# One order of the token stage for another, and one product moved from VectorE to GpSimd, in an audio tower kernel

## The reference

```python
ww = u + kt; q = maximum(pp, ww)
e1 = exp(pp - q); e2 = exp(ww - q)
y = (e1 * a + e2 * vt) / (e1 * b + e2)
ww2 = pp + w; q2 = maximum(ww2, kt)
e1b = exp(ww2 - q2); e2b = exp(kt - q2)
a, b, pp = e1b * a + e2b * vt, e1b * b + e2b, q2
```

## Time and profile before

| | us |
|---|---|
| median of 3 runs | 1123.95 (1120.25 to 1124.64) |
| the profiled execution | 1119.51 |
| its span, first to last instruction | 1117.4 |
| busy over the span: TensorE, VectorE, ScalarE, GpSimd | 947.9, 819.9, 618.0, 516.2 |
| mean granted clock of TensorE | 0.913 |

### The profile page before, as it was taken

One profiled execution on the slowest core, in us unless ns is written; L12 is line 12 of the kernel. 1 busy time (PEld: TensorE's weight loads), 2 busy tenths in 40 slices (PEclk: granted clock), 3 DMA queues, 4 the chain that ended last, 5 costly groups with the idle time before them and its releaser, 6 DMA issues. The chain is left out here.

```text
span 1117.4 us, 19101 instructions
## 1 busy us (share of the span) xinstructions
PE 947.9 (85%) x5742; PEld 791.6 (71%) x5742; DVE 819.9 (73%) x2076; ACT 618.0 (55%) x1150; POOL 516.2 (46%) x462
## 2 busy tenths in 40 slices
PE   6787788778885531999999999999999999999994
PEld 4454555445553421899899899899899899899894
DVE  2678887888877862778778778778778778778762
ACT  2766777667766512456456456456456456456441
POOL 1003443224422354257557557557557557547524
PEclk9888879887987655999999999999999999999997
DMA  9223443334211144356456456456456456456413
GB/s 295 68 85 93 126 109 97 87 100 135 89 43 29 43 43 175 118 154 168 134 147 176 132 147 173 132 146 174 132 146 174 132 148 172 134 153 168 133 25 38
DMA packets 72695, 138.98 MB, mean 124 GB/s; under 512 B 11949, under 2 KB 63790, under 8 KB 68682
## 3 DMA queue, kind: packets, MB, share of 16 engines
q0 software_dynamic: 31136, 98.34, 33.3%
q1 hardware_dynamic: 41514, 40.08, 12.8%
HBM read 110.52 MB, written 27.86 MB: 124 GB/s over the span
## 5 line engine op out<-in xcount | busy, mean ns | idle before, releaser
L1092 ACT ACTIVATE hid<-hp,b 128x512 f32<-128x512 f32 (+1 forms) x248 | 158.5, 639 | 302.8 <-PE hp L1127 295.0
L1139 PE MATMUL acc<-whi,hhi 128*128 128x256 f32 x880 | 245.9, 279 | 0.0
L1139 PE MATMUL acc<-whi,hlo 128*128 128x256 f32 x880 | 245.9, 279 | 0.0
L1139 PE MATMUL acc<-wlo,hhi 128*128 128x256 f32 x880 | 245.3, 279 | 0.0
L1223 DVE CAST hhi<-hid 128x512 fp32r<-128x512 f32 (+1 forms) x248 | 106.9, 431 | 148.4 <-ACT hid L1092 147.7
L1054 POOL DMA_INDIRECT out_rows<-yout,dest x110 | 180.0, 1636 | 63.7 <-issue 52.0
L1127 PE MATMUL hp<-xhi,whi 128*128 128x512 f32 (+1 forms) x496 | 187.8, 379 | 10.0 <-DVE xlo L1170 7.6
L1127 PE MATMUL hp<-xlo,whi 128*128 128x512 f32 (+1 forms) x496 | 184.0, 371 | 0.0
L1127 PE MATMUL hp<-xhi,wlo 128*128 128x512 f32 (+1 forms) x496 | 183.8, 371 | 0.0
L1139 PEld LDWEIGHTS acc<-wlo,hhi 128*128 128x128 f32 x880 | 165.3, 188 | 9.0
L1068 ACT ACTIVATE whi<-raw 128x512 fp32r<-128x512 f32 x248 | 154.3, 624 | 31.5 <-DMA raw<-in_ew,idx 31.5
(11 more groups left out here) (187 smaller groups left out, 1463.4 us busy)
## 6 DMA issues: line engine op xcount, KB each, us to landing
xin<-in_x SPq DMA_DIRECT2D x32, 512.0 KB
xin<-in_x SPq DMA_DIRECT2D x32, 256.0 KB
token_rows<-xs SPq DMA_DIRECT2D x16, 259.0 KB, 2.6
out_rows<-h SPq DMA_DIRECT2D x16, 256.0 KB, 2.5
token_rows<-xs SPq DMA_DIRECT2D x32, 64.8 KB, 2.4
out_rows<-h SPq DMA_DIRECT2D x32, 64.0 KB, 2.1
xg<-token_rows,tid POOLq DMA_INDIRECT x110, 2.9
out_rows<-yout,dest POOLq DMA_INDIRECT x110, 4.0
```

Source lines behind the costliest of these rows:

```text
L1092: act.activation(hid[:, c % 2, 0:j.r * P], hp[c % 2][:, 0:j.r * P], ACT.Relu, bias=b1[:, j.s, c:c + 1]).then_inc(hid_done, 1)
L1139: last = pe.matmul(acc_of(j, r), h_[:, c % 4, r * P:(r + 1) * P], w_[:, j.s, at:at + C], start=c == 0 and n == 0 and r % 2 == 0, stop=c == ...
```

## The change

- GpSimd gets the product e2sv = es[:, 1] * v, ahead of the seeds of the round and so behind the six list writes of the round before. It counts on a semaphore of its own, `product`, for which VectorE's sa scan waits. VectorE's L654 goes, and N_STATE becomes 6.
- ScalarE: the copy of conv_ps to h goes from behind kr(0) to between the clamps (dist) and xnT. The gate exponential goes ahead of kr(0). The root of p0 goes from behind lnd to between kr(1) and the root of p3.
- TensorE: kr 3 goes ahead of the transposes of xs.
- VectorE: the statistics of h (p0) go from behind div to behind t2, with up to two router steps after each of their six instructions; the shift of p0 goes behind that of p3, ahead of sb. `statistics` now calls `step` after the three aggregates too. The statistics of h1 have router steps up to 16 only, so the gate sum (step 17) comes behind the shifts.

```diff
--- before.py
+++ after.py
@@ -226,7 +226,7 @@
         tab = sem("tab")
         iotas, consts, bands, filt_done, ready = sem("iotas"), sem("consts"), sem("bands"), sem("filt_done"), sem("ready")
         setup_act, pads = sem("setup_act"), sem("pads")
-        seeded = sem("seeded")
+        seeded, product = sem("seeded"), sem("product")
         x_loaded = [sem("x_loaded0"), sem("x_loaded1")]
         h1_stored = [sem("h1_stored0"), sem("h1_stored1")]
         rows_stored = [sem("rows_stored0"), sem("rows_stored1")]
@@ -243,7 +243,7 @@
         lg_done, route, gate_exp, rank_done = sem("lg_done"), sem("route"), sem("gate_exp"), sem("rank_done")
 
 
-        N_LN1, N_LN2, N_DIFF, N_EXP, N_STATE, N_OUT, N_ROUTE = 7, 8, 2, 3, 7, 3, 25
+        N_LN1, N_LN2, N_DIFF, N_EXP, N_STATE, N_OUT, N_ROUTE = 7, 8, 2, 3, 6, 3, 25
 
         def tile_of_h(q, t):
             return h[:, bass.ds(q.at(3, t), 1), :].rearrange("p a c -> p (a c)")
@@ -329,6 +329,11 @@
             pool.wait_ge(pads, 7)
 
             def body(p0, p1, p2, p3, p4):
+                if p2:
+                    pool.wait_ge(seeded, p2.at(2, 2))
+                    pool.wait_ge(exps, p2.at(N_EXP, 3))
+                    pool.wait_ge(state, p2.at(N_STATE))
+                    pool.tensor_tensor(e2sv[:, :, :], es[:, 1], v[:, p2.s], ALU.mult).then_inc(product, 1)
                 if p1:
                     pool.wait_ge(kr_taken, p1.at(4, 2))
                     pool.tensor_tensor(kpad[:, p1.s, :, 0:1], kpad[:, p1.s, :, 1:2], c_before[:, :, :], ALU.add).then_inc(seeded, 1)
@@ -384,6 +389,11 @@
                         for k in range(HC):
                             a = slice(2 * k, 2 * k + 2)
                             act.activation(dist[:, n, a, :], dl[:, a, :], ACT.Relu, bias=bias[:, k:k + 1], scale=sign).then_inc(clamped, 1)
+                if p0:
+                    act.wait_ge(conv_done, p0.at(1, 1))
+                    act.sem_inc(act_seen, 1)
+                    act.activation(h[:, bass.ds(p0.at(3), 3), :], conv_ps[:, 0:3 * C].rearrange("p (t c) -> p t c", c=C),
+                                   ACT.Copy).then_inc(h_taken, 1)
                 if p1:
                     act.wait_ge(kr_done, p1.at(4))
                     for k in range(HC):
@@ -393,18 +403,14 @@
                     act.wait_ge(clamped, p2.at(4, 4))
                     act.activation(es[:, :, :, 1:TP], dist[:, :, :, :], ACT.Exp, scale=-1.0).then_inc(exps, 1)
                     act.activation(er[:, :, :], v[:, p2.s, :, 1:TP], ACT.Exp, scale=-1.0).then_inc(er_ready, 1)
-                if p1:
-                    kr(0)
-                if p0:
-                    act.wait_ge(conv_done, p0.at(1, 1))
-                    act.sem_inc(act_seen, 1)
-                    act.activation(h[:, bass.ds(p0.at(3), 3), :], conv_ps[:, 0:3 * C].rearrange("p (t c) -> p t c", c=C),
-                                   ACT.Copy).then_inc(h_taken, 1)
-                if p1:
-                    kr(1)
                 if p4:
                     act.wait_ge(route, p4.at(N_ROUTE, 14))
                     act.activation(ed[:, :], dm[:, :], ACT.Exp).then_inc(gate_exp, 1)
+                if p1:
+                    kr(0)
+                    kr(1)
+                if p0:
+                    root(p0, ln1, N_LN1, 6, mv1[:, :, 1], lv1, rs1, rstd1)
                 if p3:
                     root(p3, ln2, N_LN2, 7, mv2[:, :, 1], lv2, rs2, rstd2)
                 if p1:
@@ -423,11 +429,8 @@
                         act.wait_ge(t2T_done, p3.at(HC, k + 1))
                         act.activation(x2T[:, k, :], x2_ps[k], ACT.Copy).then_inc(t2T_taken, 1)
                 if p2:
-                    act.wait_ge(state, p2.at(N_STATE, 5))
+                    act.wait_ge(state, p2.at(N_STATE, 4))
                     act.activation(lnd[:, :, :], div[:, :, :], ACT.Ln).then_inc(inv_ready, 1)
-                if p0:
-                    root(p0, ln1, N_LN1, 6, mv1[:, :, 1], lv1, rs1, rstd1)
-                if p2:
                     act.wait_ge(inv_ready, p2.at(2, 1))
                     act.wait_ge(o_ready, p2.at(N_OUT))
                     act.activation(inv[:, :, :], lnd[:, :, :], ACT.Exp, scale=-1.0).then_inc(inv_ready, 1)
@@ -514,7 +517,7 @@
                     ranks(p4)
                 if p1:
                     pe.wait_ge(t1_taken, p1.at(HC, HC))
-                    for j in range(3):
+                    for j in range(4):
                         kr(p1, j)
                 if p3:
                     pe.wait_ge(xn2_ready, p3.at(3, 3))
@@ -522,8 +525,6 @@
                     pe.wait_ge(t2T_taken, p3.at(HC))
                     for k in range(HC):
                         transposes(xs[:, p3.s], x2_ps[k], t2T_done, k, False)
-                if p1:
-                    kr(p1, 3)
                 if p3:
                     pe.wait_ge(t2T_taken, p3.at(HC, HC))
                     if not p3.first():
@@ -588,6 +589,7 @@
                     dve.wait_ge(done, q.at(n, at + t + 1))
                     dve.sem_inc(stats_seen, 1)
                     dve.bn_aggr(mv[:, t, :], st[:, t, :]).then_inc(done, 1)
+                    step()
 
             def shift(q, mv, rs, nb, roots, used, done):
                 dve.wait_ge(roots, q.at(2, 2))
@@ -640,21 +642,23 @@
                     dve.wait_ge(state, p2.at(N_STATE))
                     dve.scalar_tensor_tensor(out=t2[:, :, :], in0=ey[:, :, :], scalar=CAP, in1=v[:, p2.s, :, 1:TP],
                                              op0=ALU.min, op1=ALU.mult).then_inc(state, 1)
+                if p0:
+                    dve.wait_ge(h_taken, p0.at(1, 1))
+                    statistics(p0, lambda t: tile_of_h(p0, t), st1, mv1, ln1, N_LN1, 0, lambda: route_to(min(14, routed[0] + 2)))
                 route_to(14)
                 if p3:
                     dve.wait_ge(wo_done, p3.at(1, 1))
                     dve.wait_ge(h1_stored[p3.s], p3.slot_at(48))
                     dve.tensor_tensor(h1[:, p3.s], wo_ps[:, 0:3 * C].rearrange("p (t c) -> p t c", c=C),
                                       h[:, bass.ds(p3.at(3), 3), :], ALU.add).then_inc(ln2, 1)
-                    route_on()
-                    statistics(p3, lambda t: h1[:, p3.s, t, :], st2, mv2, ln2, N_LN2, 1, route_on)
+                    route_to(15)
+                    statistics(p3, lambda t: h1[:, p3.s, t, :], st2, mv2, ln2, N_LN2, 1, lambda: route_to(16))
                 if p2:
                     dve.wait_ge(exps, p2.at(N_EXP, 3))
-                    dve.wait_ge(seeded, p2.at(2, 2))
-                    dve.tensor_tensor(flat(e2sv), e2s.rearrange("p a t -> p (a t)"), v[:, p2.s].rearrange("p a t -> p (a t)"),
-                                      ALU.mult).then_inc(state, 1)
                 if p3:
                     shift(p3, mv2, rs2, nb2, rstd2, xn2_ready, ln2)
+                if p0:
+                    shift(p0, mv1, rs1, nb1, rstd1, xn_ready, ln1)
                 route_to(19)
                 if p2:
 
@@ -662,23 +666,18 @@
                                            ALU.mult, ALU.add).then_inc(state, 1)
                     route_to(20)
                     dve.wait_ge(inv_ready, p2.at(2))
-                    dve.wait_ge(state, p2.at(N_STATE, 3))
+                    dve.wait_ge(state, p2.at(N_STATE, 2))
                     dve.scalar_tensor_tensor(out=div[:, 0, :].rearrange("p (a t) -> p a t", t=T), in0=ey[:, :, :], scalar=CAP,
                                              in1=sb_[:, :, 0:T], op0=ALU.min, op1=ALU.add).then_inc(state, 1)
                     route_to(22)
                     dve.wait_ge(er_ready, p2.at(1, 1))
                     dve.tensor_scalar(div[:, 1, :], er[:, :, :].rearrange("p a t -> p (a t)"), EMAX, 1.0, ALU.min, ALU.add).then_inc(state, 1)
-                if p0:
-                    dve.wait_ge(h_taken, p0.at(1, 1))
-                    statistics(p0, lambda t: tile_of_h(p0, t), st1, mv1, ln1, N_LN1, 0, route_on)
                 if p2:
-                    dve.wait_ge(state, p2.at(N_STATE, 2))
+                    dve.wait_ge(product, p2.at(1, 1))
                     dve.tensor_tensor_scan(flat(sa), e1s.rearrange("p a t -> p (a t)"), flat(e2sv), 0.0, ALU.mult, ALU.add).then_inc(state, 1)
                 route_to(N_ROUTE)
-                if p0:
-                    shift(p0, mv1, rs1, nb1, rstd1, xn_ready, ln1)
                 if p2:
-                    dve.wait_ge(state, p2.at(N_STATE, 6))
+                    dve.wait_ge(state, p2.at(N_STATE, 5))
                     dve.wait_ge(o_ready, p2.at(N_OUT))
                     dve.tensor_tensor(num[:, :].rearrange("p (a t) -> p a t", t=T), t2[:, :, :], sa[:, :, 0:T], ALU.add).then_inc(state, 1)
 
```

## The result

| | before | after |
|---|---|---|
| median of ten runs each | 1122.88 us (1120.25 to 1124.64) | 1128.01 us (1125.15 to 1133.63) |
| the profiled execution | 1119.51 | 1128.41 |
| its span | 1117.4 | 1126.6 |
| mean granted clock | 0.913 | 0.909 |

The ratio is 1.0051 with a 95% interval of 1.0033 to 1.0069: the kernel became slower by half a per cent. Forecast was 1093.5, range 1081 to 1113. Beside it on another chip it was 1.0066 (1.0042 to 1.0090).

A forecast was written before the change was run, and what follows sets the result against it. Waits between engines, none of them full, were taken to bound the token stage: 2.42 us off each of 12 rounds (29.0), 2.4 and 1.5 beside them, less 2.4 for holds, saved 30.5, giving 1093.5 us; range 1081 to 1113.

The forecast's parts named there:

- What bounds the kernel: Token stage: no engine is full; waits from one engine to another set each full round, 22.97 us.
- the holes before the gate sum and before num: VectorE gaps of 1.27 us before the gate sum and 1.24 before the first layer norm's shift, both expected to go.
- The two rounds beside the full ones: Rounds at 47.04 and 346.20 us, next to the twelve full ones, expected to save 2.4 and 1.5 us.
- The size of a round without any hold: Full token-stage round summed along the waits after the change: 20.55 us, down from 22.97.
- The product's price: GpSimd's product over 772 elements, in no profile row, taken as two passes: 1.6 us.
- the mild form: The product holds only the gate difference and a tiny VectorE step, both before holes: 0.2 us a round, 2.4 in all.
- rival 1: GpSimd's product starts before sel and holds a VectorE step; round about 22.0 us, total 1108.5; chance 0.30.
- a tie within 0.2 us: Product's start at 9.0 us of the round against sel's at 9.1; late list writes would put the product behind sel.
- the cast beside a fill: An 8-element cast taking 0.64 us during a fill, read as GpSimd and VectorE excluding each other.
- rival 2: Loop through conv, 19.8 us, bounds the round if TensorE's clock is low: 1100 to 1112 beyond the forecast's span, chance 0.07.
- rival 4: Nothing gained: another order of waits takes back all 2.4 us a round, total 1123; chance 0.06.
- rival 3: Slower: a GpSimd product of over 3.0 us holds sel; at 3.6 us the total is 1137; chance 0.06.

The follow-up runs named there:

- e1: The changed kernel with the product back on VectorE behind the statistics of h1, so the new order alone; 0.9725 of the kernel before, full round 21.06 us.
- e3: The changed kernel with GpSimd's product also waiting for router step 14, just behind sel; 0.9748 of the kernel before, full round 21.18 us.
- e9: The changed kernel with the product back on VectorE and a 2048-element fill in its place on GpSimd; 0.9744 of the kernel before, full round 21.08 us.
- the second trace: The changed kernel run again, unmodified, on another chip; 1.0066 of the kernel before, full round 24.32 us.
- e6: The changed kernel with GpSimd's product cut into two instructions of 386 elements each; 1.0045 of the kernel before, full round 24.14 us.
- e4: The changed kernel with router steps up to 14 ahead of the statistics of h, product still on GpSimd; 0.9684 of the kernel before, full round 20.50 us.

## Why the prediction was wrong

- **What bounds the kernel** was right: no engine is full, and a round is made by waits of one engine for another. The reordering of TensorE and ScalarE did what was said: waits for xs fell from 3.2 to at most 1.0 us and for x2T to 0.8, the holes before the gate sum and before num are gone. e1 shows what the new order is worth: 1.91 us a round. The two rounds beside the full ones gave 3.4 and 1.4, where the sum had 2.4 and 1.5.
- **The size of a round without any hold**, 20.55, was short by 0.5 (21.06 in e1, 21.18 in e3). The term is the statistics of h: I let the first one start at 6.83, right behind the end of the h copy at 6.8. The copy ends at 6.76 and the first statistic starts at 7.12, and from there to sel it is 2.45 in place of 2.27, so sel in e1 is at 9.57 in place of 9.1.
- **The product's price**, 1.6 from two passes, measured 1.80 to 1.82. The estimate of 1.7 from the figure of the Trainium skill (GPSIMD Engine Reference, section 3.1) was nearer. "So the product itself is hidden by 7 us" was true of its result and beside the point.
- **The step that failed** is that the sum let sel go unheld: its only term for the hold was the mild form, 0.2 a round, and the runs show 1.5. The place and the mechanism of rival 1 are what happened, with is_second held in ten of the twelve rounds and sel itself in two. I called it "a tie within 0.2 us", with es at 8.9 and sel at 9.1, and gave the tie to the other side, by the hope that late list writes would put the product behind sel. In ten rounds they ended at 8.3, near the 8.4 that I had also written. In the one round where they did end late, at 9.84, sel was held too, and longest of all, 2.53: by the starts in the trace, the first to start did not win there. And the error in the term above was on the same side: without the hold sel starts at 9.57, 0.5 behind the product's 9.05.
- **A row that I read too far**: the cast beside a fill was to show GpSimd holding VectorE. The cast ends 0.20 behind that fill, the holds above end within 0.06 of the product, and in e9 a fill holds no tensor_tensor. Whether a fill can hold a cast, no run here shows.
- **Rival 1 was priced too low**: "the round is about 22.0", 1108.5. With kr at full clock it was 22.57 to 22.60, which is 21.1 and 1.5 of hold. On top comes what no rival of mine had: the hold makes TensorE wait 2.6 to 3.3 us just ahead of the kr that everything else waits for, and in nine of twelve rounds (all twelve in the second trace) the granted clock was 0.50 for part or all of the first two kr. That is 23.95 - 22.60 = 1.35 a round, 16 us, the difference between a gain and the loss. My conditional in rival 2, on the lower level, looked at the loop of conv and not at kr; and "2.4 more would need kr to take twice its time in every round" in rival 4 named the number, and then took it for remote. In the kernel before the 3.2 us wait stood ahead of the transposes of xs and the fourth kr, and the trace showed that kr at 2.1 to 2.8 in place of 1.46 in nine of twelve rounds, as here in the round of the earlier trace rows:

```profile
270.39 2.13 PE L496 MATMUL kr_ps<-xnT,wr 128*128 128x384 f32 x4
```

The price of a long wait was to be read there.
- **Slower than before** (rival 3) was tied to a product over 3 us. It came with one of 1.8.
- In sum, a round: 20.55 as forecast without any hold, 0.5 for the statistics, 1.5 for the hold, 1.35 for the clock, 23.9; measured 23.95. The clock term differs from one execution to the next: it is 1.7 in the second trace, 24.32 - 22.60.

## What to carry to other kernels

A product moved to GpSimd is hidden only if the VectorE instructions that run beside it are not steps with two inputs in SBUF (or small casts and tensor_scalars) on a chain that others wait for; a 24-element step held for 1.5 us costs as much as a large one. When two events that decide a case come out 0.1 us apart in a hand count, the count decides nothing, and an explicit wait that orders them (e3, one wait, 3%) is worth more than the count. Being 0.66 us ahead by the trace was not enough either. A wait moved on TensorE has to be priced with the work behind it at half its speed, so ask what stands there.

## What the runs showed of the hardware

- GpSimd's tensor_tensor of 772 elements (two SBUF reads) takes 1.80 to 1.84, 386 elements 1.0 (e6); a fill of 2048 takes 1.81 (e9). VectorE takes 0.96 for the product.
- Under such a product VectorE's SBUF-to-SBUF tensor_tensor of 24 elements, tensor_scalar and cast of 3 elements are held to within 0.06 us behind its end; a statistic (0.43 at 240.6 in e4, under the product from 240.58), and an add with one input in PSUM (0.96 in e3), are not. Under a fill the tensor_tensor of 24 isn't held (0.18 in e9).
- A tensor_tensor of 24 elements that starts 0.66 us ahead of the product, by the trace, can be held too (2.53, the round from 90.27).
- The granted clock after a wait of TensorE doesn't follow from the length of the wait alone. In e1 and e3, waits of 1.2 to 1.7 ahead of kr left it at 2.82 or 2.83; of twelve waits of 2.6 to 3.3 in after nine were followed by 1.2 GHz for part or all of kr, and a wait of 2.60 was followed by 5.46, one of 2.92 by 2.82. The fall need not come within the wait: in six of the nine rounds the clock was 0.50 when kr began, in three it fell 1.3 to 1.4 us into kr, as this round shows, whose kr begins at 199.48:

```profile
199.48:200.48 1.00, 1.00 (x7) 0.64 (x4) 0.93 (x2) 0.20 (x1) 0.00 (x0) 1.00 0.00 0
...
201.48:202.48 1.00, 1.00 (x3) 0.66 (x2) 0.84 (x5) 0.08 (x1) 0.00 (x0) 0.50 0.62 213
```
